# Eight transformer sub-layers on one core: row statistics gathered inside the stages, and a longer first step in wide attention

## What is computed

```python
x = x + attn_a0(layernorm(x))   # 16 heads of 8, scores times a decay
x = x + moe(layernorm(x))       # 7 experts, top 2, and a shared one
x = x + attn_b(layernorm(x))    # "wide": 32 heads of 32, own layer norm at its end
x = x + moe(layernorm(x))
x = x + attn_a1(layernorm(x))   # 16 heads of 8, position bias
x = x + ffn(layernorm(x))       # integer weights, swiglu
x = x + linear(layernorm(x))    # a linear recurrence in time, own layer norm
x = x + ffn(layernorm(x))
```

## Time and profile before

| what | value |
|---|---|
| median of 3 runs (lowest, highest) | 4005.56 us (4002.24, 4005.69) |
| profiled execution: its own time, its span | 4007.65 us, 4005.9 us |
| busy: PE, PEld | 3414.4 us (85%), 2107.9 us (53%) |
| busy: DVE, ACT, POOL | 3018.0 us (75%), 2470.0 us (62%), 1207.0 us (30%) |
| mean granted clock of PE | 0.932 |

### The profile page before, as it was taken

The page is one execution under the profiler, slowest core; times in us unless marked ns, Lnnn a source line. Parts: engine busy times, 40 slices in busy tenths (PEclk is TensorE's granted clock), DMA queues, the critical chain, the costliest instruction groups (busy, mean ns, idle before and its releaser), DMA issues. The chain is left out here.

```text
span 4005.9 us, 57967 instructions
## 1 busy us (share of the span) xinstructions
PE 3414.4 (85%) x18424; PEld 2107.9 (53%) x18424; DVE 3018.0 (75%) x7074; ACT 2470.0 (62%) x4540; POOL 1207.0 (30%) x922
## 2 busy tenths in 40 slices
PE   6888888677984999999999997879699999858875
PEld 4555555465752455555545554657466666643433
DVE  7999999655864677777777774668678888659985
ACT  4888888534741565556555554457379999752324
POOL 1000000034531566666666664445300000010111
PEclk8999999878996999999999998889899999988887
DMA  4222221212435676666766661134332222200000
GB/s 136 53 50 47 54 36 20 37 41 91 146 109 86 86 90 82 90 86 85 89 82 89 87 85 20 50 109 142 108 105 47 42 34 47 36 29 0 0 1 22
DMA packets 206312, 265.36 MB, mean 66 GB/s; under 512 B 95749, under 2 KB 107334, under 8 KB 205883
## 3 DMA queue, kind: packets, MB, share of 16 engines
q1 hardware_dynamic: 196282, 240.66, 34.1%
q0 software_dynamic: 9728, 20.99, 1.6%
HBM read 102.77 MB, written 57.08 MB: 40 GB/s over the span
## 5 line engine op out<-in xcount | busy, mean ns | idle before, releaser
L1173 DVE TENSOR_REDUCE at_b_top<-ps 128x1 f32<-128x512 f32 x1024 | 661.8, 680 | 354.8 <-PE ps L923 353.8
L1062 ACT ACTIVATE at_b_e<-ps 128x512 f32<-128x512 f32 x1024 | 582.1, 599 | 472.1 <-PE ps L935 459.6
L585 ACT ACTIVATE at_a_e<-at_a_logits,at_a_neg_top 128x512 f32<-128x512 f32 x1024 | 656.1, 716 | 120.9 <-DVE at_a_neg_top L645 119.5
L822 POOL TENSOR_TENSOR at_b_e_pair<-at_b_e 128x1024 f32<-128x1024 f32 x252 | 594.3, 2378 | 396.2 <-PE ps L961 393.6
L505 PE MATMUL ps<-at_a_in_k,at_a_in_q 96*128 96x512 f32 x1024 | 476.9, 491 | 144.0 <-DVE at_a_clipped L613 117.4
L923 PE MATMUL ps<-at_b_k,at_b_q 96*128 96x512 f32 x1024 | 500.5, 492 | 41.1 <-DMA at_b_k<-at_b_k_hi 38.8
L935 PE MATMUL ps<-at_b_q,at_b_k 98*128 98x512 f32 x1024 | 423.9, 417 | 16.1 <-ACT at_b_e L1062 14.9
L641 DVE CUSTOM_DVE_ANT_0 at_a_logits<-ps,at_a_in_strip 128x512 f32<-128x512 f32 x512 | 340.6, 688 | 83.4 <-issue 33.1
L505 PEld LDWEIGHTS ps<-at_a_in_k,at_a_in_q 96*128 96x128 f32 x1024 | 184.8, 190 | 355.6 <-DVE at_a_clipped L613 206.4
L613 DVE TENSOR_SCALAR at_a_clipped<-ps 128x512 f32<-128x512 f32 x512 | 351.7, 687 | 21.1 <-PE ps L505 20.0
L455 POOL COPY at_a_v<-at_a_in_v_all 128x128 f32<-128x128 f32 x64 | 34.7, 548 | 1062.7 <-PE ps L528 1062.6
(11 more groups left out here) (340 smaller groups left out, 6489.9 us busy)
## 6 DMA issues: line engine op xcount, KB each, us to landing
moe_stage<-in_moe_w SPq DMA_DIRECT2D x46, 768.0 KB
at_b_q<-at_b_q_hi SPq DMA_DIRECT2D x128, 256.0 KB, 5.8
at_b_k<-at_b_k_hi SPq DMA_DIRECT2D x128, 256.0 KB, 7.5
at_b_q<-at_b_q_lo SPq DMA_DIRECT2D x64, 256.0 KB, 7.6
at_b_k<-at_b_k_lo SPq DMA_DIRECT2D x64, 256.0 KB, 8.0
slot_rows<-empty_slots SPq DMA_DIRECT2D x44, 288.0 KB, 5.1
moe_xg<-slot_rows SPq DMA_DIRECT2D x44, 288.0 KB
at_a_in_q<-q_hi SPq DMA_DIRECT2D x128, 64.0 KB
```

The lines of the kernel that those rows point to most:

```text
L585: act.activation(e[:, j, qb, :], logits[:, j % 2, qb, :], ACT.Exp, bias=neg_top[:, j % 2, qb:qb + 1]).then_inc(exp_done, 1)
L822: pool.tensor_tensor(e_pair[:, j, :, :], e[r][:, j, 0:2, :], e[r][:, j, 2:4, :], ALU.add).then_inc(pair_done, 1)
L1062: act.activation(e[r][:, j, b, :], g.ps[:, shifted_bank(n, b), :], ACT.Exp).then_inc(exp_done, 1)
L1173: dve.tensor_reduce(top[:, t, j, qb:qb + 1], g.ps[:, bank, :], AX_X, ALU.max).then_inc(max_done, 1)
```

## The change

The class `RowStats` takes the place of `row_stats` and `rsqrt`. A stage owns one; `take` is the `bn_stats` of a batch, `gather` its four `bn_aggr` on DVE, `root` two instructions on POOL (add eps, power -0.5) on the four numbers of the batch, `finish` a wait of POOL for the eighth root. The six phases behind the stages are gone; each stage has five semaphores of `RowStats` in place of its `stats_done`. `ffn7` takes no statistics.

```diff
+class RowStats:
+    def take(self, dve, b):
+        for tile in range((b - 1) * TB, b * TB):
+            dve.bn_stats(self.stats[:, tile, :], self.g.x_all[:, tile, :]).then_inc(self.taken, 1)
+    def gather(self, dve, b):
+        dve.wait_ge(self.taken, TB * b)
+        for tile in range((b - 1) * TB, b * TB):
+            dve.bn_aggr(self.g.mean_var[:, tile, :], self.stats[:, tile, :]).then_inc(self.gathered, 1)
+    def root(self, pool, b):
+        tiles = slice((b - 1) * TB, b * TB)
+        pool.wait_ge(self.gathered, TB * b)
+        pool.tensor_scalar(self.var[:, tiles], self.g.mean_var[:, tiles, 1], 1e-5, None, ALU.add).then_inc(self.raised, 1)
+        pool.wait_ge(self.raised, b)
+        pool.tensor_tensor(self.g.rstd[:, tiles], self.var[:, tiles], self.half[:].to_broadcast([P, TB]), ALU.pow
+                           ).then_inc(self.rooted, 1)
```

Where the calls stand. `begin`: `gather` as before, eight roots on POOL. `out_a`:

```diff
                     if n > 1:
                         take_stats(n - 1)
+                    if n > 2:
+                        rows.gather(dve, n - 2)
                 take_stats(B)
+                for n in (B - 1, B):
+                    rows.gather(dve, n)
```

The wide layer's weights move into `WideWeights`, whose buffers are open from before `moe1`, and whose twelve loads SP issues in `moe1`, behind the last expert's weights and ahead of its wait for the stored expert outputs:

```diff
                 sp.wait_ge(w_done, 3 * (SLOT_TILES + 1))
+                if wide:
+                    wide.load(sp)
                 for r in range(2):
                     sp.wait_ge(y_stored[r], y_before + 16 * TB * SLOT_TILES // 2)
```

In `attend_wide` the first three groups are projected ahead of the loop, each into PSUM banks that are free then, and groups 2 and 3 are split into parts of the still unused `e[0]`:

```diff
+        FIRST = 3
+        first_banks = ((PROJ_BANK, Y_BANK), (ST_BANK, ST_BANK + 1), (PV_BANK, PROJ_BANK))
+        def halves(n):
+            if 2 <= n <= FIRST:
+                return [e[0][:, n - 2, k, :].bitcast(F32R) for k in range(4)]
+            return [q_hi[:], q_lo[:], k_hi[:], k_lo[:]]
...
+                def project_first(n):
+                    if n == 1:
+                        pe.wait_ge(xT_done, 1)
+                    if n == FIRST:
+                        pe.wait_ge(q_lo_done, 1)
+                    for base, bank, ready in ((0, first_banks[n - 1][0], q_ready), (W, first_banks[n - 1][1], k_ready)):
+                        pe.matmul(g.ps[:, bank, :], w[:, base + (n - 1) * P:base + n * P], xT[:], start=True, stop=True
+                                  ).then_inc(ready, 1)
...
+                for n in range(1, FIRST + 1):
+                    load_q(n)
+                    load_k(n)
                 run(sp, step)
```

More of the change, by code:

```diff
@@ L142, in row_stats, with __init__, set_up, finish @@
[L142 to L162, removed]
+class RowStats:
+    def __init__(self, ph, g):
+        self.g = g
+        self.stats = ph.sb("row_stats", [P, TILES, 6])
+        self.var = ph.sb("row_var", [P, TILES])
+        self.half = ph.sb("row_half", [P, 1])
+        self.taken, self.gathered, self.half_set, self.raised, self.rooted = (
+            ph.sem(k) for k in ("row_taken", "row_gathered", "row_half_set", "row_raised", "row_rooted"))
+    def take(self, dve, b):
[5 more added lines that the diff above has]
+            dve.bn_aggr(self.g.mean_var[:, tile, :], self.stats[:, tile, :]).then_inc(self.gathered, 1)
+    def set_up(self, pool):
+        pool.memset(self.half[:], -0.5).then_inc(self.half_set, 1)
+        pool.wait_ge(self.half_set, 1)
+    def root(self, pool, b):
[5 more added lines that the diff above has]
+                           ).then_inc(self.rooted, 1)
+    def finish(self, pool):
+        pool.wait_ge(self.rooted, B)
@@ L1007, in _ @@
                 turn_x(1)
+                for n in range(1, FIRST + 1):
+                    project_first(n)
                 run(pe, step)
@@ L1035, in high, with high_first @@
                     act.activation(hi[:], g.ps[:, bank, :], ACT.Copy, scale=factor).then_inc(done, 1)
+                def high_first(n):
+                    buffers = halves(n)
+                    for k, (ready, factor, done) in enumerate(((q_ready, scale, q_hi_done), (k_ready, 1.0, k_hi_done))):
+                        act.wait_ge(ready, n)
+                        act.activation(buffers[2 * k], g.ps[:, first_banks[n - 1][k], :], ACT.Copy, scale=factor
+                                       ).then_inc(done, 1)
                 def copy_v(st):
@@ L1082, in _ @@
                 copy_x(1)
+                for n in range(1, FIRST + 1):
+                    high_first(n)
                 run(act, step)
@@ L1205, in _ @@
                 normalise(dve, g.x_all, g.mean_var, g.rstd, 1, xn, xn_done)
+                for n in range(1, FIRST + 1):
+                    low_first(n)
                 run(dve, step)
@@ L1715, in step @@
                         dve.wait_ge(x_summed, n)
-                        for tile in range((n - 1) * TB, n * TB):
-                            dve.bn_stats(stats[:, tile, :], g.x_all[:, tile, :]).then_inc(stats_done, 1)
+                        if n > 1:
+                            rows.gather(dve, n - 1)
+                        rows.take(dve, n)
                     if st.has(2):
@@ L1816, in integer_swiglu @@
+def integer_swiglu(nc, g, name, packed, w, ahead):
     C = HID // P
@@ L1964, in _ @@
                                        ).then_inc(h_lo1_done, 1)
+                    if first and n > 3:
+                        rows.root(pool, n - 3)
+                if first:
+                    for n in range(B - 2, B + 1):
+                        rows.root(pool, n)
+                    rows.finish(pool)
             @block.vector
@@ L1994, in _, with dispatch_experts @@
                                               ).then_inc(out_added, 1)
-                        if q == 2 and inside(s - 3):
+                        if first and q == 0 and inside(s - 4):
+                            rows.gather(dve, s - 4)
+                        if first and q == 2 and inside(s - 3):
                             dve.wait_ge(out_added, s - 3)
-                            for tile in range((s - 4) * TB, (s - 3) * TB):
-                                dve.bn_stats(stats[:, tile, :], g.x_all[:, tile, :]).then_inc(stats_done, 1)
-                dve.wait_ge(stats_done, TILES)
-def dispatch_experts(nc, g, name, packed, stats, slots, turn):
+                            rows.take(dve, s - 3)
+                if first:
+                    rows.gather(dve, B)
+def dispatch_experts(nc, g, name, packed, slots, turn, wide):
     C = DFF // P
@@ L2180, in _ @@
                                                 y_tok[u % 2][:, s, :], None).then_inc(y_stored[u % 2], 16)
+                rows.set_up(pool)
+                for b in range(1, B + 1):
+                    rows.root(pool, b)
+                rows.finish(pool)
             @block.tensor
@@ L2499, in _ @@
                         dve.wait_ge(added, b - 1)
-                        for t in range((b - 2) * TB, (b - 1) * TB):
-                            dve.bn_stats(stats[:, t, :], g.x_all[:, t, :]).then_inc(stats_done, 1)
-                dve.wait_ge(stats_done, T)
+                        rows.take(dve, b - 1)
+                    if b >= 3:
+                        rows.gather(dve, b - 2)
+                rows.gather(dve, B)
 class Memory:
```

339 lines of the change are left out of this document (167 added, 172 removed).

## The result

The changed kernel took 3995.15 us (median of 16 runs, 3992.12 to 3998.07) against 4003.28 us for the one before: a ratio of 0.998, 95% interval [0.9972, 0.9988], some 8 us less where 28 were forecast. A second set of runs gave 0.9976 [0.9966, 0.9987]. Its profiled execution took 3993.68 us (span 3991.8), 14.0 less than that of before; a part of these 14 is the spread between executions.

What follows compares the result with a forecast made beforehand. No engine bounds the whole kernel: PE the steady wide loop, DVE lin, waits the seams and wide layer's start. Seams -11.8, wide start -16.1, one semaphore -0.1 sum to -28.0: 4005.6 to 3977.6 us, range 3966 to 3992.

Steps and rivals of the forecast that it cites:

- the seams of moe1 and moe3: Ends of both moe stages: statistics phase gone, exit priced by semaphores cleared; -2.0 us for moe1, -2.3 for moe3.
- C: Rival at the seams: POOL's roots run as late as the old chain, 2.8 us each; total -15, 3991 us; 7%.
- Begin: Stage begin: roots at 1.40 us outlast the 1.03 between gathers, so POOL falls behind and it ends later: +2.0 us.
- out_a0, out_a1: Ends of these two stages: three roots in a row and the exit replace the statistics phase; -1.6 us each.
- ffn5: Stage ffn5: only one root exposed at its end, -3.9 us; gathers inside add +0.3; together -3.6 us.
- lin: Stage lin: -3.5 us at its end, +1.8 for six gathers in its DVE-bound loop; together -1.7 us.
- ffn7: Stage ffn7: last bn_stats and one semaphore go from its end; -0.95 us.
- Weights: Wide layer's start: weights loaded in moe1, transposes then wait only for POOL's memsets and start at +7.1; -3.6 us.
- Three groups: Wide layer's start: three groups' loads queued at once, so only transfer time, 12.6 us a group, counts; -12.5 us.
- rivals A and B: Wide layer's start: A, loads not back to back, 3984 us, 13%; B, full queue moves over 129 GB/s, 3965, 5%.
- The rest of the wide layer: Wide layer from step 4 on: each step unchanged at 18.65 us, ending on its own load; no further gain or loss.
- Rival D: Steady wide loop: any load delay is paid some 60 times; at 1.0 us a step, slower at 4038 us; 5%.

Runs made afterwards that it cites:

- early drain: Changed kernel plus one GpSimd drain in each moe, behind its last indirect DMA and ahead of its first root: 3976.26 us, 0.9939; again 3976.42 us, 0.9933.
- late memset: Kernel before the change plus one tiny GpSimd memset at each moe's end, waiting for the last batch's statistics: 4017.41 us, ratio 1.0045.
- one group: Changed kernel with one group instead of three projected and loaded ahead of the wide layer's first step: 4003.26 us, ratio 1.0009.
- after, again: The changed kernel itself, nothing edited, run again on one chip with the others: 3995.2 us, ratio 0.9976.
- e11: As e10, but twelve unread matmuls at lin's end and eleven unread 128x128 ones in ffn7 where PE waits: 3973.05 us, ratio 0.992.
- e10: Changed kernel with early drain, later wide-layer waits, fourth group projected ahead and old begin chain, plus seven unread PE matmuls behind lin's last work: 3966.59 us, 0.991.

## Why the prediction was wrong

- **The step that failed** is the seams of moe1 and moe3: "exit 3.57 + 0.26". An exit was priced by the semaphores that it clears, as if the barrier cost nothing but that. All rows behind that price come from exits at which POOL had been idle long enough. The earlier trace rows even showed it: POOL idle for 35.49 us ahead of its first memset, and its drain, to 1183.71, lay unseen in that time. Moving the roots to POOL made POOL the last to arrive, and its drain behind 152 indirect DMAs came onto the path twice: 8.65 and 8.55 us by the records, some 8.9 and 8.5 by the exits (12.63 and 12.30 against 3.77 and 3.80 with the early drain). The prediction asked what is late next at a stall that goes, but at these seams took POOL's end for the end of its roots. None of the rivals named it; C (the roots take the chain's place) had the right engine and the wrong price, for a root is 1.33 us from one to the next, as the forecast had it.
- With this one thing undone (early drain) the ratios 0.9939 and 0.9933 are 24.4 and 26.8 us below the kernel before on their chips, against the forecast's 28.0. The sum of the other terms was right within the measurement, whose interval is 5 us to either side, and partly by luck: the wide layer gave 5.6 us less than forecast and ffn7 2.2, and stages in which no term changed, or that vary by themselves, gave as much back.
- **Begin** +2.0: +1.8 by the phase lengths. Right.
- **out_a0, out_a1** -1.6 each: out_a1 -2.0; out_a0 -2 to -3, in a stage that varies by as much. Right in size.
- **ffn5** -3.6: from DVE's last statistics to lin's first work 3.84 us, before 7.85: -4.0 for the tail (forecast -3.9). The phase is 3.5 to 6 shorter; the kernel's own spread (78.4 and 75.6) hides the loop's +0.3. **lin** -1.7: measured -1.5.
- **ffn7** -0.95: +1.2 to +1.9. The term took PE's clock in the stage as given. The missing 2.2 us and more are PE at the lower clock, at the stage's start and at its end.
- **Weights** -3.6: transposes at +7.4, ended by POOL's memset, as said. **Three groups** -12.5: 12.4 at group 4. Both mechanisms, the 12.6 us of six loads and the small loads queued behind them, are as forecast (group to group 12.8 and 13.2); rivals A and B fall. The rule of the Trainium skill that the prediction set against its row ("DMA: Bandwidth & Descriptors", "Anatomy of one DMA") is given there for DMAs that GpSimd issues, and these are SP's; the row was the right guide.
- **The rest of the wide layer**, forecast "each step is what it was": true for most steps (18.5 to 18.6), but the whole layer gained 10.6 and not 16.2. From group 9's projection to the last one the layer before took 1020.4 us, after 1024.1, and behind it 1.3 more. The largest part is one step: from group 61's k projection to group 62's 21.39 us after, 18.67 before, of which the next step gave 0.6 back (18.17 against 18.79). The same step took 19.3 to 21.4 in all eleven other traces with three or four groups ahead, and 18.6 in the late memset's and in one group's. There PE waited for a load that SP had issued at its usual place in the step:

```profile
2342.95 0.50 PE L970 MATMUL ps<-at_b_k,at_b_q 96*128 96x512 f32 x1 [1.36 <-DMA at_b_k<-at_b_k_hi]
```

The DMA queues tell what stood beside that load. The queues of kind "instruction" while its last packets run, before (2356.4 to 2358.5) and after (2339.4 to 2341.5), as number of packets, MB and share of the engines' time:

```profile
q8 instruction: 1, 0.02, 5.1%
```

```profile
q8 instruction: 1, 0.02, 5.3%
q14 instruction: 2, 0.02, 3.7%
```

In all twelve traces with groups ahead a packet of q14 starts 16.1 us behind group 61's first projection, beside the one of q8 at 15.8, and the last packet of the loads ends at 18.2 to 18.8; in the three others none does, and it ends at 17.2 to 17.4. The steps of groups 33 and 47 have such a packet in the changed kernel and not before, and took 0.4 to 0.6 us more. The load is late in just the traces in which this packet runs beside its end. That the packet is the cause, and that the groups ahead only shift the loop against it, is argued from this and not shown: no run moved these packets alone.

In the profiled pair two more pieces are PE's clock. Behind the wait of 1.36 us it fell to 0.50, which cost some 1.0 us; in "after, again" it stayed at 1.00 behind one of 1.40. And the part behind the last projection took 92.7 to 93.0 us in the eight traces in which the clock falls once some 37 us into it, among them one group's, and 91.3 to 91.5 in the seven in which it doesn't, among them "after, again": the last 1.3 us have nothing to do with the change. The busy times there, after and "after, again":

```profile
2420.00:2422.00 2.00, 2.00 (x12) 0.22 (x4) 0.81 (x2) 0.00 (x0) 2.00 (x2) 0.50 0.01 2
```

```profile
2423.60:2425.60 2.00, 2.00 (x19) 0.61 (x18) 0.00 (x0) 1.98 (x4) 2.00 (x2) 1.00 0.04 6
```

Rival D (a delay in every step) is not what happened, but loads did come late in a few steps, at three of them beside such packets, which the prediction's "no instruction or order of the loop changes" does not exclude.

The sum put right: -28.0 + 17.2 (two drains) = -10.8; measured -8.1 and -9.6. In the profiled pair the wide layer's 5.6 and ffn7's 2.2 are on top, and stages that vary between executions (moe1, out_a0, ffn5, in_a1) give them back; the timings can't resolve these.

The best version here is the fourth group projected ahead with begin's chain: 0.992 [0.9907, 0.9932], and with the seven unread matmuls 0.991 [0.9894, 0.9925]; the early drain alone, one line, gives 0.9939 [0.9926, 0.9953] and 0.9933 [0.9919, 0.9946]. The first two can't be told apart, and the early drain's intervals overlap with that of the first.

## What to carry to other kernels

A barrier waits for what an engine has to finish internally, not for its last visible instruction: before work is moved onto an engine at the end of a phase, ask what that engine does there now in its idle time, and look at how long it had been idle at every exit whose price you borrow. Where GpSimd issues indirect DMAs and a phase ends soon after its last instruction, drain it once right behind them, under other engines' work. And a saving at the start of a long loop should be checked at its end.

## What the runs showed of the hardware

- POOL's drain behind indirect DMAs: 0.3 to 0.4 us behind 4, 5.3 behind 64, 7.2 behind 88, 8.3 to 9.0 behind 148 to 152, whether it comes at once or 29 us later; a second drain with none in between took 0.05.
- DVE's four `at_b_xn` took 3.77 us while POOL ran its memsets, and 1.11 us when POOL had finished: 0.94 us each against 0.28. The Trainium skill, page "SBUF — State Buffer", section "Who interferes with whom", says that a DVE instruction in a two-port mode and a GpSimd instruction exclude each other for the whole instruction. The trace agrees: two of the four ended at 1209.53 and 1209.59, just behind the first memset (1209.44), and two at 1211.42 and 1211.48, just behind the second (1211.33), thus two waits of one memset each. Whether they ran in such a mode no run here shows.
- A pause of 2.33 us on PE was followed by the lower clock level in e11, as was one of 8.16 us in e10. In the wide layer a pause of 1.36 us was followed by it in one trace, and one of 1.40 us at the same place in another was not.
- A load of the wide layer that was issued on time ended 18.2 to 18.8 us into its step where two queues of kind "instruction" had packets beside its last ones (twelve traces), and at 17.2 to 17.4 where only one had (three traces).
